# Front streams placed by tables, and two band convolutions side by side on the array

## The reference, cut to what matters

```python
x = x + L0(gn(x))   # x: (8, 256, 64, 64) fp32
x = x + L1(gn(x))
x = x + L2(gn(x))
x = x + L3(gn(x))
```

## Time and profile before

| | |
|---|---|
| median of 3 runs | 3209.29 us (3207.8 to 3211.7) |
| the profiled execution, its own time | 3209.59 us |
| span of the profile | 3207.5 us, 68136 instructions |
| mean granted TensorE clock | 0.92 |
| busy: PE, DVE, ACT, POOL | 2517.5, 2317.2, 1714.9, 1407.3 us |

### The profile page before, as it was taken

How to read it: one execution, slowest core, us unless ns; L and a number is a source line. 1 busy time by engine, 2 the same in 40 slices (tenths; PEclk the granted TensorE clock), 3 DMA queues, 4 the chain that set the end, 5 groups by cost and what they waited for, 6 DMA issues and landing times. The chain is left out here.

```text
span 3207.5 us, 68136 instructions
## 1 busy us (share of the span) xinstructions
PE 2517.5 (78%) x27316; PEld 1422.3 (44%) x27316; DVE 2317.2 (72%) x4411; ACT 1714.9 (53%) x4448; POOL 1407.3 (44%) x1052
## 2 busy tenths in 40 slices
PE   0266769897888879798888979898788969798666
PEld 0232345444544446444544446444544445444343
DVE  4968676867778786878778786877678786776433
ACT  0221066545664476645764476635765376645765
POOL 4314552456335562456335562456435452454222
PEclk9977879998999989998999979998999989999899
DMA  5300310014000321014000321014010231011100
GB/s 149 104 2 14 108 58 28 21 60 145 28 28 27 118 68 41 21 60 145 28 28 27 103 83 41 21 60 145 22 34 27 73 113 41 21 47 54 41 28 34
DMA packets 91345, 184.50 MB, mean 58 GB/s; under 512 B 37510, under 2 KB 50454, under 8 KB 80406
## 3 DMA queue, kind: packets, MB, share of 16 engines
q1 hardware_dynamic: 88854, 177.78, 16.6%
q10 hardware_dynamic: 2176, 2.36, 0.3%
HBM read 107.23 MB, written 72.86 MB: 56 GB/s over the span
## 5 line engine op out<-in xcount | busy, mean ns | idle before, releaser
L1828 PE MATMUL F<-g_raw,cw_hi 128*128 128x512 f16 x2304 | 714.3, 393 | 62.0 <-DVE ytj L1361 25.5
L821 POOL TENSOR_TENSOR xs<-xs,rec 128x512 f32<-128x512 f32 x256 | 291.2, 1142 | 911.5 <-DVE rec L1615 910.8
L1081 ACT ACTIVATE xs<-xs,mx 128x64 f32<-128x64 f32 x2048 | 513.0, 336 | 166.4 <-DVE mx L1610 166.3
L1828 PE MATMUL F<-g_raw,cw_lo 128*128 128x512 f16 x1152 | 450.7, 391 | 0.0
L1828 PEld LDWEIGHTS F<-g_raw,cw_hi 128*128 128x128 f16 x2304 | 225.6, 100 | 342.9 <-issue 35.8
L1599 DVE TENSOR_TENSOR xs<-SP,bias 128x512 f32<-128x512 f32 (+2 forms) x384 | 182.1, 502 | 199.4 <-PE SP L1904 194.7
L1872 PE MATMUL QP<-tok_hi,qkv_hi 128*128 128x512 f16 x512 | 209.0, 408 | 98.2 <-DVE tok_lo L1584 44.9
L830 POOL TENSOR_TENSOR ot_lo<-ot,ot_hi 128x512 f16<-128x512 f32 x128 | 149.3, 1187 | 263.7 <-ACT ot_hi L1102 263.7
L1334 DVE SCALAR_TENSOR_TENSOR g_raw<-l0c,gn,g_raw 128x512 f16<-128x512 f32 x192 | 199.4, 1083 | 87.3 <-ACT g_raw L965 87.3
L965 ACT ACTIVATE g_raw<-l0c,gn 128x512 f16<-128x512 f32 x192 | 128.1, 716 | 232.2 <-DVE l0c L1327 83.3
L1614 DVE TENSOR_REDUCE sums<-xs 128x8 f32<-128x512 f32 x256 | 172.0, 672 | 89.6 <-ACT xs L1081 87.7
(11 more groups left out here) (268 smaller groups left out, 5798.2 us busy)
## 6 DMA issues: line engine op xcount, KB each, us to landing
X<-in_x SPq DMA_DIRECT2D x32, 1024.0 KB, 7.2
scratch_x<-X SPq DMA_DIRECT2D x32, 1024.0 KB, 8.4
xs<-scratch_x SPq DMA_DIRECT2D x56, 512.0 KB, 3.7
out_x<-xs SPq DMA_DIRECT2D x56, 512.0 KB, 2.7
l0c<-scratch_t SPq DMA_DIRECT2D x8, 1876.0 KB, 13.6
l0c<-in_c_ind SPq DMA_DIRECT2D x8, 1024.0 KB, 6.5
l0c<-scratch_t SPq DMA_DIRECT2D x8, 640.0 KB, 15.7
l0c<-scratch_t SPq DMA_DIRECT2D x8, 576.0 KB, 16.3
```

Of the source, the lines that this page charges most:

```text
L821: G.tensor_tensor(keyed(sc[:, u % 4, :]), keyed(sc[:, u % 4, :]), rec[:, u % 4, :].unsqueeze(2).to_broadcast([P, 8, TOK]), ALU.mult).then_ ...
L1081: last = S.activation(keys, keys, ACT.Exp, bias=mx[:, u % 4, i:i + 1])
L1828: last = T.matmul(F[:, n % 2, :], wgt[:, ci, C3 * comp + dx, P * co:P * co + P], win[which], start=(ci == 0 and dx == 0 and j == 0), stop= ...
```

## The change

The front is cut into smaller pieces, and most of what need not stand in its line becomes streams with letters of their own. C is one of 16 first statistics of x (`first_stats`), U one of the 16 maxima (`maxima`), B the lower half of the lifts, J the last three additions of a unit (`joined_rows`), V its statistics and row sums (`row_sums`), all on VectorE; D is the lower half's differences and W the weighing of rows on GpSimd; H is the lower halves on ScalarE; E is what stood in norm2a to coefs, on four engines, with tiles and PSUM columns of its own (`excitation`). The front ends in one step, convend. Image 0 gets a table too, `FIRST`, and `TURN`, `AHEAD` and `LAST_ROWS` are written anew. The sums and maxima are written straight into Z. Each reduce step handles two column pairs instead of four: 16 steps, 32 hand-overs of a bank, each half as wide. The band matmuls of m = 0 and m = 1 alternate and write partitions 0 to 63 and 64 to 127 of one bank; one copy and two transposes follow instead of two and four. The group norm's second sum goes through one matmul instead of two, with one more small instruction on VectorE. m0 is kept twice. SyncE's load of an image's first row moves from norm3a into its stream of loads.

```diff
+    "SP": {"convend": "L"},
+    "POOL": {"load": "RRRR", "bands": "RR", "circ": "RR", "reduce7": "R", "reduce10": "R", "zpool": "RR",
...
+AHEAD = {"SP": {"S": 2, "L": 1}, "POOL": {"N": 4, "O": 2, "R": 24, "E": 1}, "ACT": {"X": 4, "T": 6, "Q": 6, "O": 2, "E": 1, "K": 1}, "DVE": {"S": 2, "T": 3, "A": 2, "U": 14, "E": 2}, "PE": {"Q": 3, "T": 4, "W": 4, "S": 1}}
...
-        FRONT = ([f"stats{i}" for i in range(4)] + ["norm0a", "norm0b", "norm0c"] + [f"reduce{i}" for i in range(8)]
+        FRONT = (["norm0a", "norm0b", "norm0c"] + [f"reduce{i}" for i in range(PAIRS // 2)]
...
-                 + [f"conv{n}.{i}" for n in range(UNITS * COMPS) for i in range(2)]
-                 + ["norm2a", "norm2b", "norm2c", "squeeze", "excite", "norm3a", "norm3b", "norm3c", "coefs"])
+                 + [f"conv{n}.{i}" for n in range(UNITS * COMPS) for i in range(2)] + ["convend"])
...
-                    steps.append(EARLY[name])
-                for letter in "".join(turn.get(step, "") for step in steps) if at_img else "":
+                for letter in (TURN if at_img else FIRST)[engine].get(name, ""):
...
-                        sp.wait_ge(m_dve, at(m_dve, 4 * u + 4))
+                        sp.wait_ge(x_dve, at(x_dve, u + 1))
...
-                        if f == "norm2a":
+                        if f == "convend":
                             store_x2(UNITS - 1)
                             if img + 1 < NB:
                                 sp.wait_ge(v_lo, at(v_lo, CT * 2 * COMPS))
                                 bands_to_chip(l0c_in)
                                 sp.dma_start(ind, c_ind).then_inc(l0c_in, 16)
-                        if f == "norm2b" and img + 1 < NB:
-                            fetch(UNITS - 1)
-                        if f == "norm3a":
-                            for u in range(UNITS):
-                                sp.wait_ge(x2_stored[u], 16 * (img + 1))
-                            load_row(NW * img)
...
-                    G.tensor_tensor(raw[:, t, 2 * rows + 1, :], low, high, ALU.add).then_inc(raw_sums, 1)
+                    G.tensor_tensor(Zv[:, t, rows, 1, PAD:PAD + W], low, high, ALU.add).then_inc(raw_sums, 1)
...
+                        for j in range(2 * i, 2 * i + 2):
+                            act.wait_ge(f_max, at(f_max, j + 1))
+                            if j >= 2:
+                                act.wait_ge(f_sum, at(f_sum, j - 1))
+                            S.activation(tmp[:, j % 2, 0:C], F[:, j % 2, 0:C], ACT.Copy, scale=1.0 / C,
+                                         accum_out=Z3[:, 1, 2 + j:3 + j]).then_inc(f_sum, 1)
...
-                            act.wait_ge(y_done, at(y_done, 2))
-                            for m in range(2):
-                                S.activation(yt[:, m, :], F[0:W, m, PAD:PAD + C], ACT.Copy).then_inc(y_copied, 1)
+                            act.wait_ge(y_done, at(y_done, 1))
+                            S.activation(ytj[:, 0:C], F[:, 0, PAD:PAD + C], ACT.Copy).then_inc(y_copied, 1)
...
-                        V.tensor_tensor(g_sq, g_dev, f_dev, ALU.mult).then_inc(gn_sq, 1)
+                        seq.link(V.tensor_tensor(f_dev, g_dev, f_dev, ALU.mult))
+                        V.tensor_tensor(g_sq, mv[:, :, 1], f_dev, ALU.add).then_inc(gn_sq, 1)
...
-                            V.scalar_tensor_tensor(dst[3], rows_view(ytj[:, :]), 8.0, dst[3], ALU.mult, ALU.add)
-                            V.scalar_tensor_tensor(dst[1], rows_view(ytj[:, :]), 2.0, dst[1], ALU.mult, ALU.add)
-                            seq.link(V.scalar_tensor_tensor(dst[2], rows_view(raw_flat), 4.0, dst[2], ALU.mult, ALU.add))
...
-                    for i in range(8):
-
-                        for jj in (2 * i, 2 * i + 1):
-                            dve.wait_ge(f_tr, at(f_tr, jj + 1))
-                            V.tensor_reduce(Z3[:, 0, 2 + 2 * jj:4 + 2 * jj],
-                                            F[:, jj % 2, :].rearrange("p (j c) -> p j c", j=2), AX.X,
-                                            ALU.max).then_inc(f_max, 1)
-                            last = reduce(jj)
-                            if jj == PAIRS // 2 - 1:
-                                seq.link(last)
+                    for i in range(PAIRS // 2):
+                        for j in range(2 * i, 2 * i + 2):
+                            dve.wait_ge(f_tr, at(f_tr, j + 1))
+                            V.tensor_reduce(Z3[:, 0, 2 + j:3 + j], F[:, j % 2, 0:C], AX.X, ALU.max).then_inc(f_max, 1)
...
+                def joined_rows():
+                    for img in range(NB):
+                        at = of_image(img)
+                        for u in range(UNITS):
+                            half, co, ty, px = unit(u)
+                            dst = [Xq[:, co, ty, j, :] for j in range(ROUT)]
+                            dve.wait_ge(m_dve, at(m_dve, 4 * u + 4))
+                            V.scalar_tensor_tensor(dst[3], rows_view(ytj[:, :]), 8.0, dst[3], ALU.mult, ALU.add)
+                            yield 3
+                            V.scalar_tensor_tensor(dst[1], rows_view(ytj[:, :]), 2.0, dst[1], ALU.mult, ALU.add)
+                            yield 1
+                            V.scalar_tensor_tensor(dst[2], rows_view(raw_flat), 4.0, dst[2], ALU.mult, ALU.add
+                                                   ).then_inc(x_dve, 1)
+                            yield 2
...
+                def row_sums():
+                    for img in range(NB):
+                        at = of_image(img)
+                        for m in range(CT * NCH):
+                            u, kk_ = divmod(m, 4)
+                            half, co, ty, px = unit(u)
+                            k = NCH // 2 * half + kk_
+                            dve.wait_ge(x_dve, at(x_dve, u + 1))
+                            dve.wait_ge(x_pool, at(x_pool, 2 * u + 2))
+                            V.bn_stats(stats[:, co, k, :], X[:, co, CHUNK * k:CHUNK * k + CHUNK])
+                            yield "stats"
+                            dve.wait_ge(dwt_mul, at(dwt_mul, m + 1))
+                            V.tensor_reduce(y1[:, co, ROWS * k:ROWS * k + ROWS], rows_view(tmp[:, 2 + m % 2, :]), AX.X,
+                                            ALU.add).then_inc(dwt_used, 1)
+                            yield "sum"
...
+                def first_stats():
+                    for img in range(NB):
+                        for u in range(UNITS):
+                            half, co, ty, px = unit(u)
+                            for k in range(NCH // 2 * half, NCH // 2 * half + NCH // 2):
+                                dve.wait_ge(x_in[u], 16 * (img + 1))
+                                V.bn_stats(stats0[:, co, k, :], X[:, co, CHUNK * k:CHUNK * k + CHUNK]).then_inc(stats_in, 1)
+                                yield u
+                def maxima():
+                    for img in range(NB):
+                        for t in range(CT):
+                            for kind in (1, 0):
+                                for i in range(4):
+                                    part = slice(W // 4 * i, W // 4 * (i + 1))
+                                    view = X[:, t, :].rearrange("p (h w) -> p h w" if kind else "p (h w) -> p w h", w=W)
+                                    if img == 0:
+                                        dve.wait_ge(pads_zero, 1)
+                                    for half in ((i // 2,) if kind else range(2)):
+                                        dve.wait_ge(x_in[CT * half + t], 16 * (img + 1))
+                                    V.tensor_reduce(Zv[:, t, kind, 0, PAD + W // 4 * i:PAD + W // 4 * (i + 1)],
+                                                    view[:, part, :], AX.X, ALU.max).then_inc(max_set, 1)
+                                    yield t
...
+                def excitation():
+                    for img in range(NB):
+                        at = of_image(img)
+                        def centred(n):
+                            dve.wait_ge(x_mean, at(x_mean, n + 1))
+                            V.tensor_tensor(x_dev, mv_x[:, :, 0], e_mean, ALU.subtract)
+                            seq.link(V.tensor_tensor(e_dev, mv_x[:, :, 0], e_mean, ALU.subtract))
+                            seq.link(V.tensor_tensor(e_dev, x_dev, e_dev, ALU.mult))
+                            V.tensor_tensor(x_sq, mv_x[:, :, 1], e_dev, ALU.add).then_inc(x_sqd, 1)
...
-                        m, t = divmod(i, 2)
-                        if t == 0:
-                            T.matmul(F[0:W, m, 0:C + 2 * PAD], zrow[:, 0:W], zrow[:, :], start=True, stop=False,
-                                     skip_group_check=True)
-                        for j in range(NM):
-                            last = T.matmul(F[0:W, m, P * t:P * t + BAND], Zv[:, t, m, j // KS, j % KS:j % KS + W],
-                                            toep[:, m, j, :], start=False, stop=(t == CT - 1 and j == NM - 1),
```

(44 more changed lines are left out.)

632 lines of the change are left out of this document (340 added, 292 removed), and 100 rows, old and new, of tables (FIRST, TURN).

## The result

The changed kernel takes 3004.7 us (median of 4 runs, 2996.8 to 3012.0) against 3208.6 for the kernel before beside it: 0.9368 of its time, 95% interval 0.9336 to 0.9399. The profiled execution took 3012.0, its span is 3010.1.

What follows compares the result with a forecast made beforehand. No engine was taken to bound the whole, so each stage was judged by itself. Steady images -56, image 0 -33, between image 0 and 1 +12 and tail +6 gave -71 from 3209.3: 3138 us, range 3045 to 3220.

Steps and rivals of the forecast that it cites:

- Gates and convolution stay: Steady images, logits to gates and convolution: TensorE's work is the same, moved letters only change places; no gain counted.
- its sign of being wrong: The forecast would be wrong if the gates or the convolution changed length by more than 3 us.
- Rival A: Finer pieces let the table fill 12 of 54.6 idle us per image: 7 x -12 = -84, 3054; chance 0.25.
- The bands: Band stage: the two column halves run together, halving 13.4 us per image: -6.7, bounds 0 and -6.7.
- The tables' move of two fills and a group of scores: These leave the TensorE-bound band stage for norm0 and reduce, where they cost nothing: -3.8 us per steady image.
- VectorE's term: Norm0 and reduce: 32 half-width maxima of 0.42 us in place of 16 of 0.684: +2.5 us per steady image.
- The end of the image: End of convolution to next norm0: left at 33 us, since the last fetch waits behind 12.36 us of filter issue.
- Image 0: First image: statistics moved ahead -8, bands -6.7, waits for ytj in the convolution gone -18; together -33 us.
- Between image 0 and 1: GpSimd's 28 sums ahead of its inverse root make norm0 27 us late, part comes back: +12, bounds 0 and +27.
- The tail: After the last image: two more fills and one more group of scores, 3.8 us of TensorE: +6 us.
- Rival C: Reduce steps: 32 hand-overs with half the data but the same waits, +18 per steady image, 3264; chance 0.13.
- Rival D: Bands: alternating halves costs a stop at each of 56 changes per image, +6.7 instead of -6.7, 3245; chance 0.03.

Runs made afterwards that it cites:

- e3: Changed kernel with images 1 to 7 and the tail in the order of the kernel before, the three additions inline in every image: 3277.9 us (1.0225).
- e4: Changed kernel with only the three additions of a unit back inline, ahead of that unit's last gather, in all images: 3040.3 us (0.9488).
- e8: Changed kernel with 16 hand-overs of 512 columns again in the reduce steps in place of 32, order kept: 3021.0 us (0.9411).
- e7: Changed kernel plus 72 useless matmuls ahead of norm0's first matmul in images 1 to 7: 2999.2 us (0.9338).
- e1: Changed kernel with each band piece ordered seven matmuls of m = 0, then seven of m = 1, in place of alternating: 3045.3 us (0.9499).
- e2: Changed kernel with the last fetch of x put ahead of the band filters' loads in SyncE's queue: 3007.5 us (0.9391).
- e6: Changed kernel with GpSimd's sums of image 1 spread as in later images, 4 of 28 left at the end of image 0: 3003.0 us (0.9347).
- e10: Kernel e6 with VectorE's 14 maxima of image 1 spread too, none left at the end of image 0: 2988.5 us (0.9306).
- e12: Changed kernel with only the tail in the order of before, the letters that the changed tail has more standing first: 3021.2 us (0.9424).
- e5: Changed kernel with the last fetch of x ahead of the band filters, which are issued only after step reduce5 of the next image: 2956.1 us (0.9212).

## Why the prediction was wrong

**The step that failed** is "Gates and convolution stay: TensorE's work there is the same, and each letter moved between them only changes places." The work is the same or a little more (1936 records for 1862 in image 4), and still the two stages lost 16.7 us in that image and 106 over seven. The prediction had named 3 us there as its sign of being wrong. I had read only busy time there. TensorE was idle for 23.8 us in them, in waits of 1 to 3 us for ScalarE, GpSimd and VectorE, and each ends when something that stands ahead in another engine's line is done. To move that something is what the change does. e3 shows it whole: with the pieces new and the order old both stages have their old length. e4 shows the one part of it that I cut out, the three additions, 28 us of convolution and 36 in all. How the rest divides between the attention's letters and the other small streams stays open.

Rival A named this mechanism ("finer pieces give the table more freedom") and was mis-sized, by 49 us: it had 12 of 54.6 idle us filled. The idle time of image 4 fell from 54.6 to 333.6 - 288.3 = 45.3, by 9.3, which is near it. What I had not counted is that the busy time falls too, from 307.7 to 288.3, and of these 19.4 the bands are only 6.4. The granted clock goes with that: over the six stages the time times (1 - clock) adds up to 24 us before and 15 after. A wait seems to be paid twice, once as idle time and once in slower matmuls behind it. What the slower matmuls cost is shown by the same gates at 0.94 and 1.00 (53.5 and 50.7). That waits bring the clock down is argued from rows where the two go together, as in e8, and not shown. Where another engine is nearly as busy, little of it comes back, as e7 shows.

**The bands** were right: 6.4 for 6.7, and e1 gives 41 us for all eight images. **The tables' move of two fills and a group of scores** was right: the band stage lost 12.4 us for 10.5 forecast. **VectorE's term** had the price of an instruction right, 420 ns for a 128x256 maximum, and norm0 and reduce grew by 2.3 for 2.5. That the two meet is luck: in these stages VectorE is busy for 49.5 us before and 49.0 after, since other work of it moved away, ScalarE is now busy for 41.0 of the 44.3 us of reduce, and in e8, without the term, reduce is longer. **The end of the image** was right, 32.1 for 33, and so was its reason, after a detour: e2 alone would have spoken against it.

**Image 0** was wrong: -6.4 for -33. The statistics brought norm0 6.5 earlier (44.9 for 51.4), and it was lost again at once: TensorE goes on with the transposes of reduce at 119.7 before and 119.8 after, because VectorE has the setup that lies between to do first, and no less of it. The same stretch before and after:

```profile
51.40:119.70 68.30, 3.55 (x15) 3.04 (x15) 64.08 (x158) 3.21 (x6) 11.62 (x10) 1.00 0.24 57
```

```profile
51.40:119.70 68.30, 0.67 (x4) 0.27 (x2) 65.98 (x153) 0.54 (x3) 12.40 (x9) 1.00 0.25 62
```

The stage with the bands is 3.0 us shorter where I had 6.7, and the convolution begins at 255.0 for 256.0. In it the waits for ytj did go, but one took their place. TensorE's waits there after:

```profile
PE F L1949 <- ACT tmp L999: 19.2, 1, 19.2
PE F L1949 <- DVE g_raw L1326: 5.6, 1, 5.6
PE F L1949 <- DVE X L1397: 4.6, 1, 4.6
```

That is 29.4 us, 30.3 with a last wait of 0.9, in place of the 28.7 of before. The convolution is 5.4 us shorter all the same, since TensorE's busy time fell from 106.9 to 101.2 for the same 440 records; why stays open. ScalarE's copy L999 is late because a lower half ahead of it in ScalarE's line waits for GpSimd:

```profile
316.36 1.34 ACT L1068 ACTIVATE g_raw<-l0c,gn 128x512 f16<-128x512 f32 x2 [22.92 <-POOL l0c L825]
317.60 0.67 ACT L999 ACTIVATE tmp<-F,gm 128x512 f32<-128x512 f32 x1
```

I had asked what the moved additions free, and not what is late next. **Between image 0 and 1** I had +12 for the late sums. That interval gained 4.9 where each later one gained 28.0, so the price is 23, and the reason was half right: e6 takes the sums away and nothing changes, e10 takes the maxima too and 16 us come back. I had named the engine that I saw first; VectorE was as late. **The tail** was wrong in sign, -17.8 for +6. From the end of the last convolution on it holds no more work than before (3155 records for 3160); what the list has more stood in front of the list before. Its order made it shorter, as e12 shows.

**Rival C** did not come, but its mechanism is real: it is the 13.4 us of waits in e3, and the new order is what keeps it to 8.3. **Rival D** is out by the rows of the bands. The Trainium skill (TensorEngine Tiling (Array Packing), Theoretical Speedup) says up to 2x for 64 columns; measured is 3.42 / 1.82 = 1.9.

## What to carry to other kernels

Where several in-order lines meet at semaphores, cost a reordering by the waits that TensorE has in each stage and not by its busy time: here two orders of the same pieces lay 273 us apart, against 41 us for the bands side by side. When one thing is moved out of a queue's way, read what stood behind it and now stands behind something else: the load moved forward in e2 brought nothing until the row load came along in e5. And when two engines are both late at a place, taking work from one shows nothing.

## What the runs showed of the hardware

Two fp32 matmuls of 128x64 weights and 134 columns that write partitions 0 to 63 and 64 to 127 of one PSUM bank overlap almost wholly if they alternate (1.82 us for 28 records), and hardly if seven of one half stand before seven of the other (3.02, against 3.42 in a single half). Issuing the same load of filters took 12.4 us in SyncE's queue at the end of an image, 8.6 behind the last fetch (e2), and 7.6 where e5 has it. The same 560 records of TensorE's gates took 50.7 us at a mean granted clock of 1.00 and 53.5 at 0.94, with 3.4 us of idle time in both.
